# Tokens' places numbered by partition first in two DRAM tables, and the last four tiles' expert results weighted and summed by TensorE

## What is computed

```python
logits = xf @ Wr + br
vals, idx = jax.lax.top_k(jax.nn.softmax(logits, axis=-1), 2)
w = vals / vals.sum(axis=-1, keepdims=True)
for ei in range(16):
    h = jax.nn.silu(xf @ W1[ei]) * (xf @ W3[ei])
    y = layernorm(h @ W2[ei]) * gamma[ei] + beta[ei]
    out = out + combine[:, ei:ei + 1] * y          # combine holds w where the expert is chosen
x = x + attention(xn) + out
```

## Time and profile before

| | us |
|---|---|
| median of 3 runs | 265.22 (264.67 to 266.84) |
| the profiled execution's own time | 265.45 |
| its span, first to last instruction | 263.7 |
| PE busy | 241.5 (92%) |
| DVE, POOL, ACT busy | 215.5 (82%), 198.6 (75%), 146.7 (56%) |
| mean granted TensorE clock | 0.982 of full |

### The profile page before, as it was taken

How to read it: one execution, slowest core, us unless ns; L and a number is a source line. 1 busy time by engine, 2 the same in 40 slices (tenths; PEclk the granted TensorE clock), 3 DMA queues, 4 the chain that set the end, 5 groups by cost and what they waited for, 6 DMA issues and landing times.

```text
span 263.7 us, 7199 instructions
## 1 busy us (share of the span) xinstructions
PE 241.5 (92%) x2094; PEld 211.9 (80%) x2094; DVE 215.5 (82%) x589; ACT 146.7 (56%) x496; POOL 198.6 (75%) x276
## 2 busy tenths in 40 slices
PE   1999999799999999999999999999999999999810
PEld 0666975689998999899989989997999899978600
DVE  4867998979598989797889869798988796978565
ACT  1757999595636473755454654555373756361133
POOL 8747814948888888988898899788878988866500
PEclk9999999999999999999999999999999999999975
DMA  5640698765888899779798987798878998983195
GB/s 166 198 142 4 203 337 252 239 209 166 233 254 260 240 244 296 257 227 297 230 286 217 311 277 197 247 269 275 263 210 290 282 269 223 278 248 73 63 287 157
DMA packets 68278, 60.48 MB, mean 229 GB/s; under 512 B 6544, under 2 KB 52240, under 8 KB 68240
## 3 DMA queue, kind: packets, MB, share of 16 engines
q1 hardware_dynamic: 65680, 54.78, 69.8%
q0 software_dynamic: 2560, 5.25, 6.7%
HBM read 55.22 MB, written 4.78 MB: 228 GB/s over the span
## 4 chain that ended last, share of the span: by engine, by line
PE 83%; ACT 7%; DMA 3%; POOL 2%; issue 2%; SPq 1%; DVE 1%; ACTq 0%; POOLq 0%; DVEq 0%
PE bank L990 22%; PE bank L1036 11%; PE bank L985 6%; PE bank L931 5%; ACT decay L1189 5%; PE bank L923 4%; PE bank L1032 3%; PE bank L870 3%; PE bank L789 3%; PE bank L958 3%; PE bank L913 2%; PE bank L901 2%; PE bank L875 2%; DMA decay<-res_dram 2%; PE bank L949 2%; PE bank L967 2%
## 5 line engine op out<-in xcount | busy, mean ns | idle before, releaser
L990 PE MATMUL bank<-blkT,w_up 128*128 128x128 f32 x512 | 63.2, 276 | 1.4 <-ACT blkT L1247 1.3
L990 PEld LDWEIGHTS bank<-blkT,w_up 128*128 128x128 f32 x512 | 59.9, 192 | 2.4 <-issue 1.5
L630 POOL DMA_INDIRECT blk<-xn_dram,gidx x40 | 42.4, 1060 | 16.2 <-DVE gidx L1466 8.9
L677 POOL DMA_INDIRECT res_dram<-xrow,sidx x40 | 41.3, 1034 | 11.4 <-issue 7.5
L1036 PE MATMUL bank<-w,xrow 128*128 128x128 f32 x256 | 34.7, 279 | 0.0
L1253 ACT ACTIVATE xrow<-bank 128x512 f32<-128x512 f32 x40 | 24.3, 608 | 16.7 <-PE bank L990 13.8
L1036 PEld LDWEIGHTS bank<-w,xrow 128*128 128x128 f32 x256 | 31.0, 192 | 1.8 <-issue 1.6
L669 POOL TENSOR_TENSOR rstd<-mv,mhalf 128x1 f32<-128x1 f32 x40 | 24.5, 613 | 4.9 <-DVE mv L1589 4.3
L1500 DVE SCALAR_TENSOR_TENSOR kq<-sd,rms,bias_kq 128x512 f32<-128x512 f32 x32 | 22.7, 749 | 6.7 <-issue 6.1
L1577 DVE TENSOR_TENSOR xrow<-xrow,bank 128x512 f32<-128x512 f32 x40 | 27.1, 678 | 0.6 <-PE bank L985 0.5
L1211 ACT ACTIVATE kqT<-bank 128x512 f32<-128x512 f32 x16 | 9.6, 602 | 30.7 <-PE bank L901 27.4
(11 more groups left out here) (248 smaller groups left out, 602.7 us busy)
## 6 DMA issues: line engine op xcount, KB each, us to landing
w_up<-in_L_ffn_W_dram SPq DMA_DIRECT2D x96, 256.0 KB
w<-in_L_ffn_W_dram SPq DMA_DIRECT2D x48, 256.0 KB
e_row<-e_dram SPq DMA_DIRECT2D x12, 256.0 KB, 6.1
decay<-l_dram SPq DMA_DIRECT2D x4, 512.0 KB, 5.8
gam<-in_L_ffn_gamma_dram SPq DMA_DIRECT2D x32, 64.0 KB
shift_y<-in_L_ffn_beta_dram SPq DMA_DIRECT2D x32, 64.0 KB
acc<-in_L_attn_u_dram SPq DMA_DIRECT2D x4, 256.0 KB, 3.6
xn_dram<-xrow SPq DMA_DIRECT2D x4, 256.0 KB, 5.0
```

What stands on the lines that cost most here:

```text
L630: g.indirect_dma_start(out=blk[:, b % SLOTS, :], out_offset=None, in_=xn_dram, in_offset=bass.IndirectOffsetOnAxis(ap=gidx[:, entry(b):ent ...
L677: g.indirect_dma_start(out=res_dram, in_=res[:, b % HALF, :], in_offset=None, out_offset=bass.IndirectOffsetOnAxis(ap=sidx[:, entry(b):ent ...
L990: last = m(bank[out][:, c * P:(c + 1) * P], w_up[:, u % SETS, n, c * P:(c + 1) * P], blkT[:, b % 2, :], start=True, stop=True)
```

## The change

1. **Numbering.** A token's row in both tables is now `16*p + t` (partition first). SP's write of `xn_dram`, the `iota`s that make `val`, and the loads of `res_dram` follow. One partition's four tiles of a part are then 2048 contiguous bytes in DRAM instead of four pieces of 512. Where a token sits in SBUF, the expert blocks and the output's layout stay.
2. **Parts.** `PARTS` is (0, 4, 8, 12, 16). The last part has four tiles (`LATE`) and a semaphore for each choice.
3. **Diagonals.** At the end of ACT's iterations 8, 10, 12 and 14, `weights_diagonal` makes two 128 x 128 diagonals each: the identity scaled by the token weights of one of the last four tiles and one choice, into `theta` tiles 0 to 7.
4. **The last part.** Behind everything else PE multiplies these eight diagonals with the loaded results and sums both choices in `bank[4]`; DVE adds the bank to `acc` in one instruction. ACT's weighting and DVE's per-tile instructions remain for the first three parts.
5. Three semaphores are merged into others (`spl_ready`, `spr_ready`, `L_copied`); their waits wait for the same instructions.

```diff
-        PARTS = (0, 4, 8, 13, NT)
+        PARTS = (0, 4, 8, 12, NT)
+        LATE = NT - PARTS[3]
+        DIAGONALS = {8: (0, 2), 10: (2, 4), 12: (4, 6), 14: (6, 8)}
...
-            xn_v = xn_dram.rearrange("(t p) d -> p t d", p=P)
+            xn_v = xn_dram.rearrange("(p t) d -> p t d", p=P)
...
-                    rv = res_dram[1 + k * T:1 + (k + 1) * T, :].rearrange("(t p) d -> p t d", p=P)
+                    rv = res_dram[1 + k * T:1 + (k + 1) * T, :].rearrange("(p t) d -> p t d", p=P)
...
-                    sp_.dma_start(dst[:, p0:p1, :], rv[:, p0:p1, :]).then_inc(res_in[q], 16)
+                    done = res_in[q] if q < 3 else last_in[k]
+                    sp_.dma_start(dst[:, p0:p1, :], rv[:, p0:p1, :]).then_inc(done, 16)
...
-            g.iota(val[:, 0:NT], [[P, NT]], base=1, channel_multiplier=1, allow_small_or_imprecise_dtypes=True)
+            g.iota(val[:, 0:NT], [[1, NT]], base=1, channel_multiplier=NT, allow_small_or_imprecise_dtypes=True)
...
+            pe.wait_ge(diag_ready, TOPK * LATE)
+            pe.wait_ge(f["gl_ready"], LAST + 3)
+            d = decay[:, :, :].rearrange("p t c -> p (t c)")
+            for k in range(TOPK):
+                pe.wait_ge(last_in[k], 16)
+                for j in range(LATE):
+                    lo = k * T + (PARTS[3] + j) * DM
+                    last = m(bank[4][:, j * DM:(j + 1) * DM], theta[:, k * LATE + j, :], d[:, lo:lo + DM],
+                             start=(k == 0 and j == 0), stop=(k == TOPK - 1 and j == LATE - 1))
+            last.then_inc(summed_psum, 1)
...
+            def weights_diagonal(t):
+
+                for j in range(*DIAGONALS.get(t, (0, 0))):
+                    k, u = j // LATE, PARTS[3] + j % LATE
+                    a(theta[:, j, :], ident[:, :], ACT.Copy, scale=wtop[:, k, u:u + 1]).then_inc(diag_ready, 1)
...
                 if b2 is not None:
                     silu(b2)
+                weights_diagonal(t)
...
-            for q in range(4):
+            for q in range(3):
                 weigh_results(q)
...
-            for q in range(NBATCH):
+            for q in range(3):
                 add_results(q)
+            dve.wait_ge(s["acc_done"], NT)
+            dve.wait_ge(summed_psum, 1)
+            both = acc[:, PARTS[3]:, :].rearrange("p t d -> p (t d)")
+            tt(both, both, bank[4][:, :], ALU.add).then_inc(fin_ready, 1)
```

More of the change, by code:

```diff
@@ L276, in build @@
             "var_ready", "rstd_ready", "xnA_ready", "xnV_ready", "xnT_psum", "xnT_ready", "nar_psum", "nar_ready"))
[L277 to L280, removed]
+        spt_ready, spe_ready, spu_ready, bete_ready, bet1_ready = (sem(n) for n in (
+            "spt_ready", "spe_ready", "spu_ready", "bete_ready", "bet1_ready"))
+        adt_ready, L_psum, L_exp, lrow_ready, erow_ready, bet_ready, betn_psum, omb_ready, turns_ready, theta_psum, theta_ready = (
+            sem(n) for n in ("adt_ready", "L_psum", "L_exp", "lrow_ready", "erow_ready", "bet_ready", "betn_psum", "omb_ready",
                              "turns_ready", "theta_psum", "theta_ready"))
@@ L304, in build @@
         up_in, w2_in = sems("f_up_in", SETS), sems("f_w2_in", SETS)
-        res_in = sems("res_in", 4)
+        res_in = sems("res_in", 3)
         second_ready, fin_ready, out_done = (sem(n) for n in (
             "second_ready", "fin_ready", "out_done"))
-        PARTS = (0, 4, 8, 13, NT)
+        PARTS = (0, 4, 8, 12, NT)
+        LATE = NT - PARTS[3]
+        DIAGONALS = {8: (0, 2), 10: (2, 4), 12: (4, 6), 14: (6, 8)}
+        last_in, diag_ready, summed_psum = sems("last_in", TOPK), sem("diag_ready"), sem("summed_psum")
         BY_ACT = (0, 1)
@@ L551, in _ @@
             g.iota(iota_k, [[1, NB]], base=0, channel_multiplier=0, allow_small_or_imprecise_dtypes=True)
-            g.iota(val[:, 0:NT], [[P, NT]], base=1, channel_multiplier=1, allow_small_or_imprecise_dtypes=True)
-            link(g.iota(val[:, NT:], [[-P, NT]], base=-1, channel_multiplier=-1, allow_small_or_imprecise_dtypes=True))
+            g.iota(val[:, 0:NT], [[1, NT]], base=1, channel_multiplier=NT, allow_small_or_imprecise_dtypes=True)
+            link(g.iota(val[:, NT:], [[-1, NT]], base=-1, channel_multiplier=-NT, allow_small_or_imprecise_dtypes=True))
             g.tensor_copy(val_h, val)
@@ L572, in _ @@
             g.tensor_scalar(bet_e, bet_e, 1.0, None, ALU.add).then_inc(bet1_ready, 1)
-            pool.wait_ge(spr_ready, 1)
+            pool.wait_ge(spe_ready, 2)
             link(g.tensor_tensor(sp_e, sp_e, sp_r, ALU.mult))
@@ L591, in _ @@
             pool.wait_ge(lng_ready, 1)
-            pool.wait_ge(L_copied, 1)
+            pool.wait_ge(L_exp, 2)
             g.tensor_tensor(lnw[:, :, :], lnG, L_s, ALU.subtract).then_inc(lnw_ready, 1)
@@ L1143, in _ @@
             act.wait_ge(spu_ready, 1)
-            a(sp_l, sp_u, ACT.Ln).then_inc(spl_ready, 1)
-            act.wait_ge(spl_ready, 1)
-            a(sp_r, sp_l, ACT.Exp, scale=-1.0).then_inc(spr_ready, 1)
+            a(sp_l, sp_u, ACT.Ln).then_inc(act_step, 1)
+            act.wait_ge(act_step, 2)
+            a(sp_r, sp_l, ACT.Exp, scale=-1.0).then_inc(spe_ready, 1)
             for q in range(2 * NBATCH):
@@ L1158, in _ @@
                 .then_inc(L_exp, 1)
-            a(L_s.rearrange("p t h -> p (t h)"), bank[2][:, 0:NT * NH], ACT.Copy).then_inc(L_copied, 1)
+            a(L_s.rearrange("p t h -> p (t h)"), bank[2][:, 0:NT * NH], ACT.Copy).then_inc(L_exp, 1)
             a(lrow[0:NT * NH, :], bank[2][0:NT * NH, 3 * NT * NH:3 * NT * NH + P], ACT.Copy).then_inc(lrow_ready, 1)
```

## The result

The changed kernel takes 266.36 us (median of 17 runs, 265.36 to 267.93), the kernel before 265.38 beside it (17 runs, 264.34 to 266.84). The ratio is 1.0046, with a 95% interval of 1.0027 to 1.0064: 1.2 us slower, 0.7 to 1.7 (the two medians alone differ by 1.0). By the 1% bound that is the same; the loss is small and real. The forecast was 265.3 and no difference.

The account below looks back on a forecast made before the run. PE's list was taken to bound the loop, so only the tail could gain: 265.45 - 0.2 (DVE's end) + 0.2 (store) + 0.1 (loop) = 265.55, 265.3 us on the median's scale; range 263.4 to 266.6.

Parts of the forecast that it names:

- What bounds the kernel: Whole kernel: PE's own list sets the loop's time, and the change can win only in the tail.
- The diagonals' products: PE, tail: sixteen instructions at half clock take 3.6 us from the seventh load's landing; DVE ends 0.2 us sooner.
- Rival B: PE in the tail: PE isn't late and DVE's list bounds the tail, 263.4 to 264.6 us; chance 0.22.
- The loads: Eight result loads, tail: longer runs cut 7.3 us to 6.4; evenly spaced, the seventh lands at 256.7, the eighth at 257.6.
- rival A: Result loads in the tail: they get no faster, DVE ends 0.6 us later than now, 266.1 us; chance 0.15.
- Two of the signs: Tail: eighth load 0.5 to 1 us sooner after the first than 7.3; DVE's last sum about 12.5 after the last scatter's landing.
- rival C: Eight result loads: the new 8 KB stride slows them, at half the rate 272.3 us; chance 0.05.
- DVE's parts: DVE in the tail: three parts of four tiles at 2.0 us each, 6.0 in all, and a final sum of 0.68.
- The store: Last store, tail: 256 KB instead of 192 lands in 2.3 us instead of 2.1, plus 0.2.
- The diagonals in the loop: ACT, loop: a pair takes about 0.6 us, squares come 0.2 late within 0.35 of slack; 0.1 us, bounds 0 and 2.4.
- Rival D: ACT, iterations 8 to 14: making the diagonals holds up the loop, up to 2.4 us, 267.6 us; chance 0.10.
- The numbering, elsewhere: Gathers and scatters at other addresses: zero, between 0.3 us better and 0.3 us worse for the one scatter on the chain.

Follow-up runs that it names:

- by parts: Changed kernel with row 512*(t//4) + 4*p + t%4, so each part's 2 KB runs are adjacent, 256 KB in one piece: 1.0008 of the kernel before.
- filler: Changed kernel plus 23 unread products on PE between its last attention product and the diagonals' products, keeping PE busy: 0.9980 of the kernel before.

## Why the prediction was right or wrong

**What bounds the kernel: right.** The loop is PE's list, unchanged, and the whole difference lies in the tail.

**The diagonals' products: right, and the step the forecast rested on.** 3.6 us from the seventh landing were forecast, 3.40 measured and 0.14 until their start. PE's clock was at the lower level, as the earlier trace rows had it for the same idle time, and rose again for the last three instructions only; in two kernels where it didn't rise they took 3.75. DVE's wait of 1 to 2 us was 1.92. That the clock sets the products' time was an argument then and is shown now, by two kernels that keep PE from being idle in different ways (2.02 us both times). Rival B, PE not late, fell with it.

**The loads: wrong, and this is the step that failed.** "I scale the 7.3 us by 292/331 = 0.88 and get 6.4", and from it the seventh load at 256.7, 8.2 us after the first issue. It landed after 9.1. Three things were mis-sized in that term. The first landing came 2.9 us after its issue, not 2.7 (0.2 of the 0.9). The time for the other seven was 6.9, not 6.4 (0.4 for the seventh). And the even spacing was wrong (0.3): the changed kernel's loads land at 2.9, 3.6, 4.5, 7.0, 6.8, 8.5, 9.1 and 9.8 us, and behind the third nothing lands for 2.4 us. Even spacing fits the kernel before, whose loads do land nearly evenly (2.7, 4.0, 5.2, 6.3, 7.3, 8.8, 8.8 and 10.0), as they do by parts; the hole, of 2.1 to 2.4 us, is in all four traces with the change's numbering and the loads in this order. The seventh is what PE starts on, and it gained nothing. The last landings of before and after differ by 0.1 (9.95 and 9.8). With the seventh 0.9 later than in the sum, DVE's end would have been 0.7 above before's instead of 0.2 below: the tail measures 0.74. With that term, the 0.2 for the store and 0.1 for the loop the working gives 265.45 + 0.7 + 0.3 - 0.23 = 266.2, and 266.36 was measured. That is rival A's time (266.1), to which I gave 0.15; that the time still lies within the range is owed to A's place in it, not to the forecast's sum. Two of the signs said so too: the eighth load was to land 0.5 to 1 us sooner than 7.3 us after the first and came 0.4 sooner, and DVE's last sum was to end about 12.5 us after the last scatter's landing (247.54) and ended 13.6 after it.

Rival A was right in its time and only half in its reason. It held that the rate of 331 GB/s came from rows that are read many times over, so that runs of 2 KB would gain nothing. The numbering by parts shows that they gain: 5.5 us instead of 7.3. What took the gain away in the change was the stride, rival C's place and cause at a fraction of its price: 6.9 - 5.5 = 1.4 us, not a doubling. I had both mechanisms and treated them as alternatives, when here they worked against each other.

The Trainium skill, "DMA: Bandwidth & Descriptors", section "Latency and other measured facts", has 207 GB/s at a row pitch of 512 KiB, 164 at 2 MiB, and the half that the prediction speaks of (103) at 4 and 8 MiB only, against 214 with a padded pitch. By these rows a pitch of 8 KB would cost nothing; here it costs 6.9 us against 5.5. Why it does, these runs don't show. The same page's section "Specifications" has 512 B enough for line rate; by that the adjacent runs of 2 KB could not have gained, and the measurement says that they did (334 GB/s from first to last landing against 251, 1,792 KB in 5.5 and 7.3 us). The measurement decides.

**DVE's parts: right.** 2.0 us each, three parts and a sum of 0.69, as forecast. But DVE was idle for 1.42 us ahead of the second part, which the even spacing had hidden; PE's lateness covered it.

**The store: right in sign.** 2.3 us to landing, 0.2 more than before.

**The diagonals in the loop: 0.1 forecast, 0 measured.** A pair takes 0.69 us, and at the start of iteration 9 the idle 0.42 of the earlier trace rows is gone. These are ACT's rows there in the changed kernel:

```profile
155.07 0.69 ACT L1238 ACTIVATE theta<-ident,wtop 128x128 f32<-128x128 f32 x2
...
156.34 0.27 ACT L1195 ACTIVATE rot<-bank 128x128 f32<-128x128 f32 x1
```

The squares start at 156.34, 0.19 later than before, but PE's own list is 0.14 later in this execution, so the delay is 0.05. `norm_kq` comes 0.14 later, that is not at all. Rival D fell.

**The numbering, elsewhere, and the merged semaphores: zero, right.** The numbering alone is at 1.0006, and the last scatter lands in 2.23 us as before. The semaphores had no run of their own; nothing in the trace points to them.

## What to carry to other kernels

PE, handed work at the end of a kernel, brings the clock it has by then: products for it after a microsecond or more without work should be priced at the lower level (3.4 to 3.75 us here instead of 2.0), and they pay only if something else is still running for as long. Longer DMA runs were one half of the layout here, the distance between them the other: the loads gained when each read one contiguous piece. And if a step starts on the seventh of eight transfers, ask when that one lands, since a mean rate doesn't say.

## What the runs showed of the hardware

- Loads of 2 MB in eight pieces into 128 partitions, all profiled executions. Runs of 512 B, each tile contiguous (five): 261 to 283 GB/s between 3 and 8 us after the first issue, the last landing after 9.9 to 10.4. Runs of 2 KB at 8 KB distance (five): 286 to 320 GB/s, 9.4 to 9.8. Runs of 2 KB adjacent (four): 331 to 349 GB/s, 8.1 to 8.3. The DMA engines' mean share in these windows is 0.90 to 1.02, 0.86 to 0.91 and 0.90 to 1.01: it doesn't put the layouts in order. Why the distance slows the loads stays open.
- Loads of one queue don't land in their order: in the changed kernel the fifth landed before the fourth, by 0.1 to 0.2 us, with the numbering alone the seventh before the sixth (8.4 and 8.8 us after the first issue).
- SP's issues got quicker with fewer runs: eight in 3.7 to 4.2 us instead of 5.6 to 5.9. In the changed kernel the landings didn't follow.
- The sixteen instructions took 2.0 us at a granted clock of 1.00 (2.23 where they had to wait for the eighth load) and 3.4 to 3.75 where most or all of them ran at the lower level.
- How long PE keeps the full clock without work isn't fixed. With the numbering alone its last product ended at 251.26 and the clock fell 1.0 us later; with the diagonals made and not used it ended at 251.53 and the clock fell 3.9 us later. The windows before and behind the fall, of the one and of the other:

```profile
251.30:252.20 0.90, 0.00 (x0) 0.00 (x0) 0.90 (x4) 0.74 (x3) 0.00 (x0) 1.00 0.66 209
252.30:263.00 10.70, 0.00 (x0) 0.00 (x0) 6.42 (x18) 4.17 (x14) 0.00 (x0) 0.50 0.66 209
...
251.60:255.40 3.80, 0.00 (x0) 0.00 (x0) 2.81 (x9) 2.08 (x7) 0.00 (x0) 1.00 1.06 276
255.50:263.00 7.50, 0.00 (x0) 0.00 (x0) 4.58 (x13) 2.83 (x10) 0.00 (x0) 0.50 0.73 200
```

All other traces without filler lie between: PE, idle since its last attention product, lost the clock after 1.0 to 3.1 us. So the two kernels with PE's loads in front, full clock after 0.18 us without work and just losing it after 1.63, are single observations and give no limit.
